# Third attention layer: scores, exponentials and weights placed one step earlier, an image's projections packed into six steps

## The reference

```python
# x: (B=8, C=256, N=1024), nh = 8 heads of hd = 32
h = groupnorm(x) * norm_w + norm_b            # 32 groups
qkv = (h.transpose(0, 2, 1) @ qkv_w.T + qkv_b).reshape(B, N, 3, nh, hd)
q, k, v = qkv[:, :, 0], qkv[:, :, 1], qkv[:, :, 2]
attn = softmax(einsum('bnhd,bngd->bnhg', q, k) * hd ** (-0.5))   # 8x8 for each pixel
o = einsum('bnhg,bngd->bnhd', attn, v).reshape(B, N, C)
return x + (o @ proj_w.T + proj_b).transpose(0, 2, 1)
```

## Time and profile before

| | |
|---|---|
| three runs before, us | 1884.17, 1877.64, 1884.83; median 1884.17 |
| the profiled execution, us | 1881.66; its span from first to last instruction 1879.9 |
| PE, DVE, ACT, POOL busy in the span | 88%, 73%, 42%, 72% |
| mean granted TensorE clock | 0.945 of full speed |
| the last attention layer | from about 1480 us to the end, some 400 us |

### The profile page before, as it was taken

How to read it: one execution, slowest core, us unless ns; L and a number is a source line. 1 busy time by engine, 2 the same in 40 slices (tenths; PEclk the granted TensorE clock), 3 DMA queues, 4 the chain that set the end, 5 groups by cost and what they waited for, 6 DMA issues and landing times.

```text
span 1879.9 us, 37124 instructions
## 1 busy us (share of the span) xinstructions
PE 1657.9 (88%) x15160; PEld 768.5 (41%) x15160; DVE 1375.4 (73%) x2121; ACT 790.8 (42%) x1542; POOL 1361.0 (72%) x581
## 2 busy tenths in 40 slices
PE   5898666799999999999999999999999988989975
PEld 2333223344344344444444444444444545555541
DVE  5777577887777777777777777777776257878875
ACT  0443410155455445545545545545546533333320
POOL 0684500198788788788788788788788758988996
PEclk8898887799999999999999999999999989999996
DMA  5000030310001001001001001001001121222211
GB/s 193 1 2 1 1 132 0 113 52 24 2 1 69 2 2 69 2 2 68 2 2 69 2 2 69 2 2 68 2 2 69 30 88 48 82 74 76 68 59 48
DMA packets 48431, 75.10 MB, mean 40 GB/s; under 512 B 30804, under 2 KB 31110, under 8 KB 48262
## 3 DMA queue, kind: packets, MB, share of 16 engines
q1 hardware_dynamic: 38758, 72.15, 10.8%
q10 hardware_dynamic: 9504, 0.59, 0.3%
HBM read 44.87 MB, written 25.17 MB: 37 GB/s over the span
## 4 chain that ended last, share of the span: by engine, by line
PE 58%; DVE 31%; issue 4%; ACT 3%; POOL 2%; DMA 1%; POOLq 0%; SPq 0%; ACTq 0%; DVEq 0%
DVE MX L1371 19%; PE AV L697 8%; PE RB L776 6%; PE AV L785 3%; PE S L733 3%; PE S L645 3%; PE RB L733 3%; PE RB L1015 2%; DVE HI L1348 2%; DVE LO L1349 2%; PE RB L723 2%; PE RB L751 1%; PE S L751 1%; POOL PR L1307 1%; PE S L994 1%
## 5 line engine op out<-in xcount | busy, mean ns | idle before, releaser
L1281 POOL TENSOR_TENSOR ACC<-ACC,PR 128x1024 f32<-128x1024 f32 x360 | 843.9, 2389 | 24.9 <-ACT PR L1143 24.7
L1143 ACT ACTIVATE PR<-S 128x512 f32<-128x512 f32 x682 | 385.9, 603 | 382.1 <-PE S L683 273.9
L1371 DVE TENSOR_REDUCE MX<-S 128x1 f32<-128x512 f32 x661 | 431.6, 680 | 107.8 <-PE S L645 50.7
L1281 POOL TENSOR_TENSOR ACC<-PR 128x1024 f32<-128x1024 f32 x72 | 169.6, 2378 | 354.9 <-PE S L712 156.5
L697 PE MATMUL AV<-PR,VT 128*32 128x512 f32 x2304 | 304.1, 606 | 2.0 <-ACT PR L1143 2.0
L645 PE MATMUL S<-HI 32*128 32x512 f32 x661 | 259.1, 481 | 17.9 <-DVE MX L1371 11.7
L1143 ACT ACTIVATE PR<-RB 128x512 f32<-128x512 f32 x320 | 190.0, 602 | 102.5 <-PE S L683 41.6
L1371 DVE TENSOR_REDUCE MX<-RB 128x1 f32<-128x512 f32 x298 | 199.8, 679 | 25.9 <-PE RB L645 13.2
L668 PE MATMUL S<-HI 32*128 32x512 f32 x682 | 193.4, 465 | 2.4 <-DVE X L1564 2.3
L645 PEld LDWEIGHTS S<-HI 32*128 32x128 f32 x661 | 105.8, 187 | 188.7 <-DVE MX L1371 83.0
L1307 POOL TENSOR_TENSOR PR<-WO,WRK 128x1792 f32<-128x1792 f32 x32 | 155.5, 4877 | 27.4 <-DVE ENC L1723 18.1
(11 more groups left out here) (362 smaller groups left out, 3466.2 us busy)
## 6 DMA issues: line engine op xcount, KB each, us to landing
X<-out_y SPq DMA_DIRECT2D x24, 1024.0 KB, 5.1
out_y<-X SPq DMA_DIRECT2D x16, 1024.0 KB, 5.1
X<-in_x SPq DMA_DIRECT2D x8, 1024.0 KB, 8.3
OHU<-out_y SPq DMA_DIRECT2D x8, 512.0 KB, 4.2
X<-out_y SPq DMA_DIRECT2D x8, 512.0 KB, 4.2
out_y<-X SPq DMA_DIRECT2D x8, 512.0 KB, 3.1
out_y<-OHU SPq DMA_DIRECT2D x8, 512.0 KB, 3.3
WO<-WO SPq DMA_DIRECT2D x128, 16.0 KB, 1.9
```

The lines of the kernel that those rows point to most:

```text
L1143: nc.scalar.activation(exps(s, pair)[:, HALF * one:HALF * one + HALF], RING[ring.place()], ACT.Exp, scale=1.0 if i is None else float(D) * ...
L1281: nc.gpsimd.tensor_tensor(ACC[:, pair, :], so_far, exps(s, pair), ALU.add).then_inc(pool_used, 1)
L1371: nc.vector.tensor_reduce(out=MX[:, h, t, keys:keys + 1], in_=bank(), op=ALU.max, axis=AX.X).then_inc(ring_free, 1)
```

## The change

Three things move in the loop of the last layer; no instruction is added or left out in what is computed.

1. `scores3` goes from PE's steps 3 and 7 to steps 2 and 6; `centre` from the end of DVE's steps 0 and 4 to the end of steps 3 and 7 before them; `exp3` from ACT's steps 1 and 5 to 0 and 4; `weigh` from DVE's steps 1 and 5 to 0 and 4.
2. Within its step `weigh` stands behind `outputs(n)` where it stood ahead of it.
3. `FRONT_UNITS` puts the eight units into steps 0 to 5 with two in step 3 and two in step 4, where before they filled steps 0 to 6 with two in step 5. Steps 6 and 7 have none now.

```diff
-FRONT_UNITS = ((0,), (1,), (2,), (3,), (4,), (5, 6), (7,), ())
+FRONT_UNITS = ((0,), (1,), (2,), (3, 4), (5, 6), (7,), (), ())
...
-                    if 0 < b < B and k == 3:
+                    if 0 < b < B and k == 2:
                         scores3(b, 1)
                     if b < B - 1:
-                        if k == 7:
+                        if k == 6:
                             wait(pe, ring_free, posted)
                             scores3(b + 1, 0)
                         front_v(b + 1, k)
...
-                    if 0 < b < B and k in (1, 5):
+                    if 0 < b < B and k in (0, 4):
                         exp3(b, k // 4)
...
-                    if 0 < b < B and k in (1, 5):
-                        weigh(b, k // 4)
                     if 0 <= n < TILES:
                         outputs(n)
+                    if 0 < b < B and k in (0, 4):
+                        weigh(b, k // 4)
                     if 0 <= n + 1 < TILES:
                         products(n + 1)
-                    if 0 < b < B and k in (0, 4):
-                        centre(b, k // 4)
+                    if 0 < b < B and k == 3:
+                        centre(b, 1)
+                    if b < B - 1 and k == 7:
+                        centre(b + 1, 0)
```

## The result

The changed kernel takes 1919.89 us (median of four runs, 1917.66 to 1920.23), the kernel before, with one more run beside it, 1883.35 (1877.64 to 1884.83). The ratio is 1.020 (95% interval 1.0182 to 1.0218), so about 37 us or 2.0% slower; 1918 was forecast (1916 for a run like the one profiled). The profiled execution took 1920.13 us (span 1918.3, mean granted clock 0.944).

The account below looks back on a forecast made before the run. PE's list plus its round trips to ACT bounds the kernel: 1881.66 + 30 (26.5 + 1 + 4.2 - 1.7) + 4.5 for the clock = 1916 us like the profiled run, forecast 1918, range 1893 to 1932.

Parts of the forecast that it names:

- round trips and moved work: PE's steps, images 1 to 5: waits for ACT and moved work add 5.3 us an image, +26.5.
- clock behind the new lull: PE idle some 2.2 us in step 7: three clock drops in images 1 to 5, +7 us.
- disturbance of image 3, gone: Image 3: its earlier drop to 1.2 GHz may go away, -2.5 us.
- image 0, image 6 and the tail: Outside images 1 to 5: image 0 +1, image 6 +4.2, image 7 -1.7 us.
- step 3: PE, two units and no scores: 7.7 us against 6.0, +1.7.
- step 4: PE, a second unit adds 2.99 us to 4.41: 7.4 us, +3.0.
- step 5: PE, one unit instead of two: 4.93 us, -3.0.
- steps 6 and 7: PE, no units; transpose waits for `keep_v`, values for `keep_o` behind `apply3`: 10.65 us against 9.57, +1.1.
- step 2: PE, the score block of 2.49 us moves in: 4.93 + 2.5 = 7.4 us.
- the rival in which the clock stays down: Steps 7, 0 and start of 1 at 1.2 GHz, about 5.5 us an image: 1937 us, chance 0.11.
- The rule of the Trainium skill: PE's short pauses between PSUM-cycling matmul groups swing the clock: a drop in each image, 1921 us.
- The rival of the ring: POOL and DVE set the pace; `weigh` behind `outputs` and early scores remove POOL's waits: 1870 us, chance 0.08.

Follow-up runs that it names:

- the split: Kernel before, with the second unit of step 5 behind that step's transpose and output projection on PE and ACT: 1873.72 us, ratio 0.9966.
- the new units alone: Kernel before with nothing but the new `FRONT_UNITS`: 1900.31 us, ratio 1.0105.
- the filler run: Changed kernel with four unread matmuls on PE ahead of step 7's values in images 1 to 5: 1912.76 us, ratio 1.0170.
- the old units: Changed kernel with the former `FRONT_UNITS` put back, scores still a step early: 1903.11 us, ratio 1.0117.
- the split in the changed kernel: Changed kernel with the second unit of steps 3 and 4 behind the transpose and projection: 1898.70 us, ratio 1.0107.
- the covered kernels: Kernel before, step 5's second unit and units of steps 0 and 4 behind the transpose: 1868.83 us; with `weigh` behind `outputs` too: 1878.45 us.
- `apply3` behind `keep_o`: Changed kernel with `apply3` of images 1 to 5 moved on ACT to between `keep_o` and `keep_v` of step 7: 1904.33 us, ratio 1.0126.
- `apply3` made short: Changed kernel with `apply3` for images 3 to 7 normalising 8 of 1024 pixels, rest left out: 1899.89 us, ratio 1.0106.

## Why the prediction was right

**PE's list and its round trips to ACT set the pace.** Shown: shortening only them in the kernel before, with no matmul less, made it faster (the split, by 0.3%), and lengthening them made it slower (the new units alone). PE has no wait for DVE in images 1 to 6 of the kernel after.

**The sum.** From the first scores behind image 0 to those five images later the kernel before took 218.55 us and the one after 252.25, +33.7; I had 26.5 + 4.5 = 31. The parts, worked out from starts:

| over five images, us | predicted | measured |
|---|---|---|
| round trips and moved work | +26.5 | +30.8 |
| clock behind the new lull | +7 | +9.0 |
| disturbance of image 3, gone | -2.5 | -6.1 |
| image 0, image 6 and the tail | +3.5 | +1.2 |
| the layer | +34.5 | +34.9 |

The first row is what is left of the +33.7 when the next two are taken out. It fits the two images of the filler run in which the clock did not fall: 48.59 us, 6.1 over the 42.48 before, five times 6.1 is 30.6.

Step by step the sizes held: step 3 7.75 us (7.7 predicted), step 4 7.38 (7.4), step 5 4.93 (4.93), steps 6 and 7 10.91 (10.65), step 2 7.61 (7.4). The wait of the values behind `apply3` was 2.24 us for "some 2.2", and step 6's transpose did wait for `keep_v` (0.56). The prediction left out one wait: at full clock step 0's values wait 1.73 us for `keep_o` behind the new lull, where they waited 1.25 before. With 0.3 us more in steps 6 and 7 and 0.2 in step 2 that makes about 6.1 us an image for the 5.3 of the sum.

**The clock was mis-sized, and so was what goes away.** I took three falls at 2.3 us. It fell behind the lull in all five images. Values to values over steps 7 and 0 took 7.47, 7.47, 6.15, 6.33 and 7.46 us. With the same lull and a full clock they take 5.18 (seen twice with the old units and once with the split in the changed kernel), so the falls cost 2.3, 2.3, 1.0, 1.2 and 2.3, in all 9.0: the price of a long fall was right, their number was not, and two were short. That it fell every time is not a property of the lull: behind the same 0.56 and 2.24 us it fell in three of five images with the old units and in four of five with the split. It was back at full speed in step 1 each time, so the rival in which the clock stays down did not come.

The rule of the Trainium skill that the prediction named ("TensorE: Matmul & The Clock Gate", "A second HAM failure mode: psum-queue depth-cycling"), as the prediction read it, would have the drop in each image, and gave 1921; the trace of the changed kernel agrees on these five drops. It does not agree as a rule about pauses of this kind in general: in steps 3 and 4 of the kernel after there are four pauses of 0.82 to 1.41 us within 12 us, every unit behind them takes 1.93, and three of fifteen lulls of 2.24 us had no drop.

On the other side, image 3 had lost 5.6 us before (48.06 from scores to scores, for 42.48), 0.5 more went in other images, and both are gone: I had counted only the 2.5 of the clock, and not the stall of 2.36 us among the score matmuls ahead of it. That stall is in image 3 of all seven kernels whose scores stand in steps 3 and 7 (1.94 to 2.36 us), with a fallen clock behind it, and in none of the six with the scores a step early. Why it is tied to that place is open.

So the sum came out by luck as well: 4.3 us too little for the round trips and 2.0 for the clock, 3.6 too much left in image 3 and 2.3 too much at the ends.

**The ends.** From the layer's start to the first unit of image 1 it took 0.6 us less than before, for the predicted +1. The next two steps took 2.0 us less, because the clock was down for longer there before; that was not in the sum. The other +3.8 lie in images 6 and 7, for +2.5. In image 7 POOL's waits for `outputs` fell from 1.95 us (0.44, 0.84 and 0.67) to a single one of 1.27, 0.7 us for the predicted 1.7. I did not take image 6 apart.

**The rival of the ring** was wrong for this kernel, as its own condition said: it decides only if PE's steps add up to less than before. In the covered kernels they do, and there `weigh` decides: moved behind `outputs`, it takes away their whole gain.

## What to carry to other kernels

Where an engine leads whose copies are made by another, count its round trips, not only its instructions: a second pass through a single PSUM bank costs nothing if a transpose and a projection stand between, 0.6 to 0.9 us with the transpose alone, and 1.05 to 1.4 with nothing. Before work is moved out of a place, ask what wait it covers there, and what stands ahead of the awaited instruction in the other engine's list: the scores covered a copy that was queued behind 2.4 us of normalisation. And a wait that disappears from an engine that does not lead (POOL's 30.6 us) may have been exchanged for another of the same size; look at all its waits before calling it gained.

## What the runs showed of the hardware

- PE stood for 0.56 us, worked for 0.4 and stood for 2.24, in five images of each of three kernels: the clock fell behind it in five, three and four of them. A fall cost 1.0 to 2.3 us. With 0.56 in place of the 2.24, and 0.95 a little later, it fell in one of five (`apply3` behind `keep_o`); with 0.56 alone (`apply3` made short) in none. With filler work and a wait of 1.81 us in the next step it fell in three of five, in step 1. What tells the images of one kernel apart was not found.
- PE stood for 1.94 to 2.36 us within the scores of image 3, waiting for nothing that the profile shows, in all seven kernels that had the scores in steps 3 and 7, each time with six of the 128 small matmuls left. It was gone in the six kernels with the scores one step earlier.
- The part of the program that was the same in all kernels took between 1498.68 and 1503.43 us, a run of each. For differences of that size the layer's own length tells more than the kernel's time, and the length of its images more than the layer's.
- Eight small transfers, started one after the other by SP, took 5.05 us to start, and 8.2 us passed from the end of `weigh`, which made their data, until POOL used them.
